# Moving units of a streamed pass from VectorE to ScalarE and GpSimd (preactivation convolution and bias, one core)

## The reference

```python
# layer 0: masked (lower triangle) depthwise 6 x 11 convolution of the normalised input
xm = jnp.where(causal_mask, x, 0)
y = conv(xm, weight[:, None, :, :], padding=((5, 0), (5, 5)), feature_group_count=16)
x = x + jnp.where(causal_mask, y, 0)          # _L0_conv_ref(_gn(x), weight)
# layer 1: normalised x plus a bias that depends on channel and (row - column)
h = relu(pos @ W1 + b1); h = relu(h @ W2 + b2); table = h @ W3 + b3
x = x + (_gn(x) + transpose(table[row - column + n - 1]))
# _gn: 8 groups of 2 channels, mean and variance over the whole group
```

## Time and profile before

| | before |
|---|---|
| median of 3 runs | 2648.5 us (2640.96 to 2651.2) |
| the profiled execution | 2642.3 us, its span 2640.6 us |
| busy | DVE 87%, PE 75%, PE weight load 70%, ACT 63%, POOL 48% |
| moved by DMA | 901 MB, mean 341 GB/s |

### The profile page before, as it was taken

The page is one execution under the profiler, slowest core; times in us unless marked ns, Lnnn a source line. Parts: engine busy times, 40 slices in busy tenths (PEclk is TensorE's granted clock), DMA queues, the critical chain, the costliest instruction groups (busy, mean ns, idle before and its releaser), DMA issues. The chain is left out here.

```text
span 2640.6 us, 76787 instructions
## 1 busy us (share of the span) xinstructions
PE 1967.7 (75%) x28880; PEld 1861.1 (70%) x28880; DVE 2296.1 (87%) x4175; ACT 1659.4 (63%) x3051; POOL 1256.5 (48%) x1988
## 2 busy tenths in 40 slices
PE   4289988877688886878788777888868787899700
PEld 0289887777687776877777776787768777888700
DVE  7799988899888997899898998989988899878745
ACT  2167766767567575666667566666657667687722
POOL 1123235535545454463555445554554546575543
PEclk9999999999889989989898999999989999999955
DMA  9775639999899999999999998999989998798899
GB/s 339 268 242 173 233 133 371 394 368 357 322 399 386 379 334 348 396 354 387 349 347 392 353 374 326 382 391 372 347 328 412 369 379 295 291 355 313 316 410 366
DMA packets 316250, 901.17 MB, mean 341 GB/s; under 512 B 42416, under 2 KB 42416, under 8 KB 314000
## 3 DMA queue, kind: packets, MB, share of 16 engines
q1 hardware_dynamic: 199648, 579.79, 59.5%
q10 hardware_dynamic: 116416, 319.37, 31.0%
HBM read 579.50 MB, written 319.68 MB: 341 GB/s over the span
## 5 line engine op out<-in xcount | busy, mean ns | idle before, releaser
L1162 PEld LDWEIGHTS psY<-wsplit,XT 128*128 128x128 f16 x25920 | 1590.0, 101 | 361.1 <-DVE XT L780 120.6
L1162 PE MATMUL psY<-wsplit,XT 128*128 128x168 f16 (+5 forms) x25920 | 1619.1, 222 | 293.6 <-DVE XT L780 241.0
L639 ACT CAST XT<-psT 128x512 f16<-128x512 f32 x720 | 415.1, 577 | 555.0 <-PE psT L1148 318.4
L1088 POOL COPY halo<-XT 128x16 f16<-128x16 f16 x720 | 314.7, 437 | 656.6 <-DVE XT L780 646.8
L780 DVE TENSOR_TENSOR XT<-psT,XT 128x512 f16<-128x512 f32 x720 | 493.4, 685 | 145.0 <-ACT XT L639 144.0
L1062 POOL TENSOR_TENSOR xn<-xn,mask 128x512 f32<-128x512 f32 x336 | 424.0, 1262 | 391.3 <-ACT xn L627 330.4
L808 DVE BATCH_NORM_STATS2 entries<-ring 128x6 f32<-128x512 f32 x872 | 551.3, 679 | 60.3 <-DMA ring<-in_x 59.9
L1148 PE MATMUL psT<-ident,xn 128*128 128x128 f32 x2880 | 480.4, 292 | 106.1 <-POOL xn L1062 87.5
L1097 POOL TENSOR_TENSOR ring<-ring,bias 128x1024 f32<-128x1024 f32 x184 | 416.4, 2265 | 270.4 <-ACT ring L687 270.2
L627 ACT ACTIVATE xn<-kept_c_band,normp 128x512 f32<-128x512 f32 (+2 forms) x496 | 398.4, 803 | 49.9 <-DMA kept_c_band<-in_x 31.9
L1148 PEld LDWEIGHTS psT<-ident,xn 128*128 128x128 f32 x2880 | 318.0, 146 | 116.1 <-POOL xn L1062 80.2
(11 more groups left out here) (78 smaller groups left out, 471.9 us busy)
## 6 DMA issues: line engine op xcount, KB each, us to landing
ring<-in_x SPq DMA_DIRECT2D x628, 512.0 KB, 8.7
out<-ring ACTq DMA_DIRECT2D x288, 512.0 KB, 6.5
kept_c_band<-in_x SPq DMA_DIRECT2D x224, 512.0 KB, 7.9
out<-kept_c_band ACTq DMA_DIRECT2D x224, 512.0 KB, 7.3
band<-in_x SPq DMA_DIRECT2D x48, 1024.0 KB, 11.3
out<-band ACTq DMA_DIRECT2D x48, 1024.0 KB, 8.8
ring<-out SPq DMA_DIRECT2D x96, 512.0 KB, 9.4
bias<-bias_scratch SPq DMA_DIRECT2D x16, 1793.5 KB, 8.7
```

The costliest lines, as they stand in the source:

```text
L639: nc.scalar.copy(XT[:, n % NB3, 0, :, 2:P + 2], psT[n % NB3][:, :, :]).then_inc(hi_ready, 1)
L1088: nc.gpsimd.tensor_copy(halo[:, t, :, :, :], XT[:, n % NB3, :, :, P:P + 2]).then_inc(halo_out, 1)
L1162: last = nc.tensor.matmul(psY[m][:, 0:rows, o + lo_c:o + hi_c], XT[:, m, xp, i, 2 - sh:2 - sh + P], wsplit[:, c, wp, K * sh:K * sh + rows, ...
```

## The change

One line changes: the rule that gives a unit to DVE.

```diff
-    U_ON_DVE = lambda n, u: n > 85 or (u % 2 == 1 if n > 78 or 36 < n < 42 else u % 4 == 3)
+    U_ON_DVE = lambda n, u: n > 85 or u % 2 == 1 and 28 < n < 42
```

## The result

The changed kernel takes 2670.5 us (median of 4 runs, 2665.9 to 2672.7), the kernel before 2644.7 (4 runs), so it is slower: ratio 1.0095, 95% interval 1.0078 to 1.0111, some 25 us. The profiled execution of the changed kernel took 2665.9 us, its span 2664.2, against 2640.6 before.

The account below looks back on a forecast made before the run. It took transfers to bound steps 9-36 and 51-68, VectorE step 74, and GpSimd's work to limit the group's end; 6 x (0 - 1.0 + 0.0) + 2.0 = -4.0 us, forecast 2645 us, range 2635 to 2657.

Parts of the forecast that it names:

- signs of being right: VectorE some 70 us less busy, full pass within 2 us of 313, transfer-bound steps unchanged, step 74 6.0 us, GpSimd over 24.
- Stage 8: Near group 0's length, which has no units; VectorE idles 46 us there, so fewer units on it give nothing.
- Units 9 and 13: Steps 29 and 35: unit 9 free, unit 13 ends step 40's 2.77 us stop; -1.0 a pass, cost at most 1.27.
- Units 3, 7 and 19: Steps 7, 21, 51, at or in transfer-bound stretches: 0 a pass, bounds -3.8 and +2.2.
- The lock: Rival, chance 0.06: moved units' GpSimd adds hold up VectorE's kept halves, 2.2 us a pass slower, 2658 us in all.
- Unit 23: Step 74, where VectorE works alone: its whole instruction is on the path, -2.15 us a pass.
- Units 27 to 33: Steps 79 to 85: ScalarE's scale +1.15, unit 31's add on GpSimd +1.99, shorter mask -0.99 us a pass.
- The sum of the last two: Step 74 and group's end: -2.15 + 1.15 + 1.99 - 0.99 = 0.0 a pass, bounds -3.45 and +3.9.
- Stage 9: Last stage: unit 27's store stands behind one more GpSimd add, +2.0 us, bounds 0 and 3.1.
- the ring that comes round too late: Rival, chance 0.21: unit 27's later store brings unit 31's load 3.9 us late at the group's end; 2668 us.
- VectorE's time is kept: Rival, chance 0.32: at the group's end 5.4 us a pass is saved; 2612 us, or 2589 if early units count.

Follow-up runs that it names:

- run 4: Kernel before with only units 9 and 13 moved to VectorE (steps 29 and 35): ratio 1.0042.
- run 5: Kernel before with only unit 13 moved to VectorE (step 35): ratio 1.0043.
- Runs 9 and 10: Kernel before with stores of units 14-17 and 27-30 cut to 16 columns in six full passes, 0.9949; the same plus unit 13 on VectorE, 0.9931.
- run 3: Kernel before with only units 3, 7 and 19 moved off VectorE (steps 7, 21, 51): ratio 1.0013.
- run 2: Kernel before with only unit 23 moved off VectorE (step 74): ratio 0.9971.
- run 1: Kernel before with only units 27, 29, 31 and 33 moved to ScalarE and GpSimd (steps 79 to 85): ratio 1.0041.
- run 18: Kernel before with small stores (units 14-17, 27-30), small adds (units 30, 32), and units 27, 29, 31, 33 off VectorE: 0.9919, or 1.0035 to its base without that move.
- run 15: Kernel before with units 23, 27, 29, 31 and 33 together moved off VectorE: ratio 1.0041.
- run 13: Kernel before with GpSimd adding the bias of units 30 and 32 to the first 16 columns only: ratio 0.9956.

## Why the prediction was wrong

It said 2645 us and no change that can be measured; it is 25 us slower. Both bounds that it set on the whole were right (the full pass does not follow VectorE, and GpSimd is short of time at the group's end). Its signs of being right came true nearly all: VectorE's 70 us less, steps 9 to 36 and 51 to 68 within 0.7 us, step 74 at 6.0 us, GpSimd busy over 24 us, and the pass that it looked at kept its length (the mean of the six windows grew by 2.5). None of them names steps 35 to 46, where most of the loss is.

By place, the two traces differ by 23.6 us, where the prediction had -4, so it missed these by 27.6. Steps 35 to 46 are 2.2 us a pass longer where it had -1.0: 19 us of the miss. Stage 8 is 6.4 longer where it had nothing. Steps 74 to 89 are 0.5 a pass longer where it had 0.0: 3 us. The rest, with group 0's 2.3 us less, is -1. Term by term, its own working against the runs:

- **Units 9 and 13: -1.0 a pass, -6 us. This step failed.** Measured +11 us (1.0042), nearly all of it unit 13's. The stop of step 40 did go, and steps 35 to 40 are 1.2 us shorter in run 4, so even the -1.0 is there. The mistake was to book it as kept. I had called this stretch bound by transfers, and a stop for a load in such a stretch is only where the queue of loads and stores shows. Unit 13 on VectorE, 2.40 us in step 35, makes that step 1.9 us longer and ScalarE's stores behind it later, and unit 14's then takes longer to land as well. The next loads wait for those stores, and VectorE stands for them in steps 41 and 46, where it has no slack. I bounded the net cost at 1.27 us, the instruction's own length; by run 5's ratio it was 1.9 us a pass. Runs 9 and 10 bear it out: with the stores small, the stops of steps 41 and 46 are gone and unit 13 costs nothing that can be measured, though the lighter traffic may have its part in that.
- **Units 3, 7 and 19: 0.** Measured +3 us (1.0013), near enough. The lock's 2.2 us a pass, a rival here, are not there: by the trace of run 3 the passes are 1.0 us shorter each, and what is lost is in stages 8 and 9 (3.0 and 1.7 us). That trace is of the fastest of 12 executions, its span 1.2 us shorter than before's, so it says little of where the loss is.
- **Unit 23: -2.15 a pass, -13 us. Half of it was wrong.** Step 74 falls by 2.07 in every trace, to 6.0 us as forecast. But run 2 gains only 8 us. In its trace steps 75 to 85 give back 1.2 a pass (this execution was the slowest of 12 and gained nothing in all, so the size of that is rough). VectorE is early there and stands for the ring; its rows in run 2, ScalarE's scale of unit 28 and VectorE's unit 29:

```profile
1594.37 1.15 ACT L687 ACTIVATE ring<-ring,outp 128x1024 f32<-128x1024 f32 x1 [3.10 <-DMA ring<-out]
...
1599.07 1.28 DVE L980 SCALAR_TENSOR_TENSOR ring<-ring,outp,bias 128x1024 f32<-128x1024 f32 x1 [2.28 <-DMA ring<-out]
```

- **Units 27 to 33: 1.15 + 1.99 - 0.99 = +2.15 a pass and +2 at the end, +15 us.** Measured +11 (1.0041). That the size came out is luck, and the mechanism was only a part: in place of 2.15 in every pass, run 1's trace has 0.5 on average in five of them, 7.8 in the last full pass, and 4.7 in stage 8, where I had nothing. The chain of GpSimd's adds is there: it is busy 28.73 of 31.40 us from unit 26's add to the mask of step 86 (forecast over 24 of 26.90). But beside it stands the ring's turn, and behind both the lock: each removal left the loss at 0.35% to 0.48% and brought another wait to the front. That the lock holds the rest up is read from run 18's rows; no run took it away. I had these as rivals of which one would hold, and the rows show all three at the same place.
- **The sum of the last two, 0.0 a pass.** Measured +0.5 in steps 74 to 89 of the whole change. I added unit 23's gain to the group's end as if step 74 were a place of its own. By the times it isn't: in run 15 nothing of unit 23's 8 us is left. By the marks most of it is still there, so where those 7 us go stays open.
- **Stage 8: nothing. This step failed too.** It is 8.7 us longer by its window, 6.4 from mark to mark. That VectorE idles there says that taking work from it gives nothing; I didn't ask what the work costs where it goes. In steps 75 to 89 of that stage the whole change and run 1 alone both lose 2.5 us, so that part belongs to the four units. In steps 60 to 69 run 3 loses 3.4, after a gain of 1.8 in steps 40 to 59. What holds it up there, and why the last full pass can't make up its end, stays open; no run was made for it.
- **Stage 9: +2.0.** Measured +2.0.

So the parts make -8 + 3 + 11 + 11 = 17 us of the 25 measured. The 7 us that unit 23 loses beside the end would nearly close the gap, but both are about as large as their uncertainty. Of the rivals, the ring that comes round too late had the right sign and nearly the total (2668), but not the place, so its total is luck as well: it was priced for unit 31 in step 83, and the wait shows for unit 34 in step 86 and for the statistics of steps 41 and 46. Its mark in the changed kernel's trace is the growth of L808's idle time from 60 to 90 us. VectorE's time is kept in step 74, and in part in steps 75 to 85 of the first five full passes, where it pays for most of the loss behind them.

The lock took part in it. The Trainium skill (SBUF — State Buffer, section "SBUF: two separate sides") says that the loser of the shared port pair stands until the other's instruction ends. Run 18 bears it out: unit 33's add ends at 1595.68, and unit 34, begun at 1593.81, ends 1.09 us behind it, so it had done next to nothing of its 1.27 us by then.

The best of the versions that compute everything is run 2, unit 23 alone off VectorE: 0.9971 (0.9961 to 0.9981), 8 us less than before.

## What to carry to other kernels

A wait for a load in a stretch that is bound by transfers is not a gain to be booked: here, removing it let two loads go ahead of a store, the wait moved to later loads, and since the edit also made the engine that issues the stores later, it came back longer. Where an edit moves work to an engine with room on average, price it at the places where that engine is in front of the critical chain, and don't add the gains of neighbouring places before a run has both together. Compare pass by pass before taking means: most of run 1's loss was in the last full pass and the stage behind it. When taking one limit away does not bring the time back, take the suspected ones away together, against a base that has them away too, before you believe that the theory was wrong.

## What the runs showed of the hardware

Relieving GpSimd of 3.5 us a group at its end made the kernel 0.44% faster by itself (run 13), 12 us for 8 x 3.5 = 28 us of work, on the engine that the page of the profile shows as the idlest (48%). A VectorE unit that began 0.13 us behind a GpSimd add took 2.96 us in place of 1.27, and two adds in one row 4.31 us where two undisturbed take 3.98. The median of a ring store rose from 6.5 to 6.9 us with the same bytes moved; no run was made for why.
